# Gated cross-attention with a routed expert layer: bias add ahead of row sends, other send batches, plan pieces, normalisation by slot, products first

## The chip, the cores and the metric

The kernel runs on one core of a Trainium2 chip. The metric is device time in microseconds (us), the median of repeated runs, lower is better. A profile is one further execution, recorded by the hardware profiler; it has a span (first to last instruction) and its own device time. Engines: TensorE (PE, with PEld for its weight loads), VectorE (DVE), ScalarE (ACT), GpSimd (POOL), and SyncE (SP), which only issues transfers.

## The reference

For 32 sequences of 128 rows and 128 columns (float32):

```
x  = x + tanh(g0) * xattn(ctx, layernorm(x), mask)     # 8 heads of 16; ctx is 32 x 128 x 256
x  = x + tanh(g1) * ffn(layernorm(x))
xattn: k, v from ctx (W_src), q from layernorm(x) (W_tgt), softmax(q k / 4) v with the mask,
       then [layernorm(x), update] @ W_out + b_out
ffn:   router of 8 experts, softmax, top 2 (weights renormalised), h = gelu(x @ w1[e]) (512 wide),
       y = h @ w2[e], sum of the two experts' y with their weights
```

The expert layer computes for each row only its two experts. Rows are therefore sorted by expert at run time.

## The kernel before, in words

**Two stages, one program.** The attention works through 32 sequences in 8 groups of 4. A step (g, k), g from 0 to 12 and k from 0 to 3, advances every stage of the pipeline by one sequence: the sequence of a stage is n = 4g + k - LAG, with lags from 4 (projections) over 5 and 6 (scores), 7 (products of the values, `LAG_PV`) to 8 (the outputs' transposes, `LAG_O`). Work per group follows at group lags: 3 (output projection, second layernorm), 4 (router), 5 (`LAG_SEND`: sends). The expert stage is a list of 71 slots of 128 rows of one expert each: transpose (slot n), first product (n + 2), second product (n + 4). Steps up to (9,1) run alone; from (9,2) on (`MIXED`) each step is followed by 2 or 3 slots (`PER_OF`): (9,2) by slots 0 to 2, (9,3) by 3 to 5, (10,0) by 6 to 8, and so on; the rest of the slots follow alone.

**Order.** Each engine has its own instruction list in program order, written by a function `step` (and `slot`) per engine; semaphores are the only connection. An instruction that waits holds up all that stands behind it on its engine.

**One step on TensorE** (L1495 on): transposes of the outputs of one sequence (L1501), transpose and projections of another (L1510 to L1528), at k = 0 the ranks of a routed group (L1428 to L1445), the turn of the row maxima (L1493), and then at k = 0 the transposes of the second layernorm's rows (L1540, into `ps_tail`, which must wait until VectorE has read the ranks: its instruction `before`, L1064) and of the attention outputs (L1550); at k = 1 the output projection (L1557), at k = 2 the router (L1566). The products of the values (L1581) and the score block (L1460 to L1479) end the step. The turn waits for both maxima of the step (L1247: first of the far half of the heads, then, after `rsum` and `on`, of the near half); the near one overwrites a buffer that ScalarE's exponent (L751) of the sequence before must have read.

**ScalarE** copies results out of PSUM (kT L788, vals L791, x2nT L799, onT L805, oT L812), takes the exponents, normalises (L745 first, L739 second layernorm), and in the expert stage copies xt (L846) and applies GELU (L855).

**GpSimd** builds the key blocks (L595, L598), computes rs and mr of both layernorms (L605 to L618), adds the output bias to the group's rows of `xs` (L642; for the first group L624) for which VectorE's residual add (L1310) of the next step waits, makes the mask's penalties (L634), and issues the sends: for each group 8 indirect transfers (L657) that scatter its rows into the experts' regions of `rows` in DRAM, `scatter(G, sends)` with batches of two per step by the table `SENDS`: sends 0 and 1 at (G+5, 1), 2 and 3 at (G+5, 2), 4 and 5 at (G+5, 3), 6 and 7 at (G+6, 0). At k = 3 the bias add stands behind the sends. The groups 5 to 7 are sent from slots. Results go back by further indirect transfers (L675).

**The plan.** VectorE computes at run time which slot serves which expert, in three stages: slots 0 to 24 from the first four groups, 25 to 40 from six, the rest from all. `first_plan` has five pieces, one each at (8,0), (8,1), (8,2), (8,3), (9,0); piece 2 (`pass_ends`) is L1120 and L1124, piece 3 (`sum_up`) L1136 and L1137. SyncE issues the slots' loads (`xg`, L543): load 0 needs the first plan and all sends of the groups 0 to 3.

**Second layernorm.** `normalise_again(G, ...)` gives four instructions on ScalarE at (g, 3), ahead of the near exponent; for group 7 alone (`AHEAD`, g = 10) they are issued one by one in the slots 14 to 17. L1540 of the next step needs all four.

Of the kernel before, what the change touches and what calls it, by code (L numbers as in the profile page):

```python
# [10 lines left out]
ALU = mybir.AluOpType  # L11
# [4 lines left out]
T = 128  # L16
# [57 lines left out]

SENDS = (range(6, 8), range(0, 2), range(2, 4), range(4, 6))
KQ = 4
BOXES = 3
# [32 lines left out]

AHEAD = (10, 2)
PAIRS_AT = (5, 11, 12, 13, 15, 17, 22, 24, 26)
# [21 lines left out]
def sequence(g, k, lag):  # L134

    n = GROUP * g + (k - lag)
    if isinstance(n, int) and not 0 <= n < BATCH:
        return None
    return n


def group(g, lag):
    n = g - lag
    if isinstance(n, int) and not 0 <= n < GROUPS:
        return None
    return n
# [20 lines left out]
def gated_cross_attention_moe(nc, x, ctxT, mask, weights, vectors, w1, w2, ident_c, tables_c,  # L167
                              integers_c, rows, picked, out):
    with ExitStack() as stack:
# [409 lines left out]
        def _(pool):  # L579
# [6 lines left out]
            def step(g, k):  # L586
# [32 lines left out]
                G = group(g, 0)  # L619
                if k == 3 and G == 0:  # L620
                    if isinstance(g, int) and g == 0:
                        pool.wait_ge(s_setup, 3)
                    pool.wait_ge(s_xn, GROUP * G + GROUP)
                    nc.gpsimd.tensor_tensor(  # L624
                        xs[:, bass.ds(GROUP * G, GROUP), :], xs[:, bass.ds(GROUP * G, GROUP), :],
                        bout_g[:, :].unsqueeze(1).broadcast_to([128, GROUP, D]),
                        ALU.add).then_inc(s_xb, 1)
# [9 lines left out]
                if G is not None and G <= STAGES[0]:  # L637
                    scatter(G, SENDS[k])
                G = group(g, 0)
                if k == 3 and G is not None and G > 0:  # L640
                    pool.wait_ge(s_xn, GROUP * G + GROUP)
                    nc.gpsimd.tensor_tensor(  # L642
                        xs[:, bass.ds(GROUP * G, GROUP), :], xs[:, bass.ds(GROUP * G, GROUP), :],
                        bout_g[:, :].unsqueeze(1).broadcast_to([128, GROUP, D]),
                        ALU.add).then_inc(s_xb, 1)

            def scatter(G, sends):

                i = outbox(G)[0]
                if sends[0] == 0:  # L650
                    pool.wait_ge(s_pos, POS * G + POS)
                    pool.wait_ge(s_rt, ROUTE * G + ROUTE)
                    pool.wait_ge(s_xr, G + 1)
                    settled()
                for t in sends:
                    pick, b = divmod(t, GROUP)
                    nc.gpsimd.indirect_dma_start(  # L657
                        out=rows, out_offset=bass.IndirectOffsetOnAxis(
                            ap=posi[:, i, pick, b:b + 1], axis=0),
                        in_=xr[:, i, pick, b, :], in_offset=None).then_inc(s_send[i], 16)  # L660
# [50 lines left out]
        def _(act):  # L711
# [37 lines left out]
            def exponent(n, banks, heads_of, done):  # L749
# [4 lines left out]
                    bias=pencol[:, bass.ds(n, 1)]).then_inc(done, 1)  # L754

            def step(g, k):
                n = sequence(g, k, LAG_PROJ)
# [26 lines left out]
                if n is not None:  # L784
                    act.wait_ge(s_proj, n + 1)
                    wait(act, s_kblkr, n - 3)
                    wait(act, s_kblk, n - 3)
                    nc.scalar.activation(kT[:, (k - LAG_PROJ) % KQ, :], ps_proj[:, 0:T], ACT.Identity,  # L788
                                         bias=bkey).then_inc(s_k, 1)
                    wait(act, s_pv, n - 3)  # L790
                    nc.scalar.activation(  # L791
                        vals[:, (k - LAG_PROJ) % 4, :, 0:HD],
                        ps_proj[:, 2 * T:3 * T].rearrange("p (h c) -> p h c", c=HD),
                        ACT.Copy).then_inc(s_v, 1)
                G = group(g, LAG_ROUTE)
                if k == 0 and G is not None:
# [9 lines left out]
                if k > 0:  # L806
                    copy_maxima(g, k)
                n = sequence(g, k, LAG_PV)
                if n is not None:
                    act.wait_ge(s_pv, n + 1)  # L810
                    wait(act, s_o, n)
                    nc.scalar.activation(flat(oT[:, :, :]), ps_o[:, 0:2 * T], ACT.Copy).then_inc(s_oT, 1)  # L812
                G = group(g, 0)
# [7 lines left out]
                G = group(g, LAG_OUT)  # L821
                if k == 3 and G is not None and g != AHEAD[0]:
                    normalise_again(G, range(GROUP))
# [17 lines left out]
            def slot(n):  # L841
# [10 lines left out]
                if j is not None:  # L852
# [3 lines left out]
                                         ACT.Gelu).then_inc(f_gelu, 1)  # L856
                b = n - slot_at(*AHEAD) - 2
                if 0 <= b < GROUP:
                    normalise_again(AHEAD[0] - LAG_OUT, (b,))
                G, late = divmod(n - ADD_FROM - 3, 2)  # L860
# [19 lines left out]
        def _(dve):  # L880
# [371 lines left out]
            def step(g, k):  # L1252
                n = sequence(g, k, LAG_SCORE + 1)
                if n is not None:
                    dve.wait_ge(s_sc, n + 1)
                    if n == 0:
                        dve.wait_ge(s_zero, 3)
                    highest(n, FAR, s_max_far)
                n = sequence(g, k, LAG_O)
                if n is not None:  # L1260
# [11 lines left out]
                n = sequence(g, k, LAG_SCORE + 1)  # L1272
                if n is not None:
                    wait(dve, s_exp_near, n)
                    highest(n, NEAR, s_max)
# [54 lines left out]
                if k == 2 and G is not None:  # L1330
                    parts[:] = routing(G)
                    parts[0]()
                piece = {(8, 0): 0, (8, 1): 1, (8, 2): 2, (8, 3): 3, (9, 0): 4}.get((g, k))
                if piece is not None:
                    first_pieces[piece]()
# [67 lines left out]
        def _(pe):  # L1403
# [81 lines left out]
            def turn_maxima(g, k):  # L1485

                n = sequence(g, k, LAG_ST)
                if n is not None:
# [5 lines left out]
                                        ident[:, :]).then_inc(s_maxTp, 1)  # L1494

            def step(g, k):
                n = sequence(g, k, LAG_O)
# [34 lines left out]
                if k == 0:  # L1532
                    turn_maxima(g, k)
                G = group(g, LAG_ROUTE)
                if k == 0 and G is not None:
# [33 lines left out]
                if k > 0:  # L1569
                    turn_maxima(g, k)  # L1570
                n = sequence(g, k, LAG_PV)
                if n is not None:
                    r = (k - LAG_PV) % 2
                    if isinstance(n, int) and n == 0:
                        pe.wait_ge(s_pool0, 1)
                    pe.wait_ge(s_exp, n + 1)
                    pe.wait_ge(s_v, n + 1)
                    wait(pe, s_on, n)
                    for h in range(HEADS):
                        q = h % QUADS  # L1580
                        last = nc.tensor.matmul(  # L1581
                            ps_o[VPAD * q:VPAD * (q + 1), (h // QUADS) * T:(h // QUADS + 1) * T],
                            vals[:, (k - LAG_PV) % 4, h, :], probT[:, r, h, :], start=True, stop=True)
                    last.then_inc(s_pv, 1)
                n, m = sequence(g, k, LAG_SCORE), sequence(g, k, LAG_ST)
# [105 lines left out]
```

## Time and profile before

| | |
|---|---|
| runs | 326.61 us median of 3 (326.29 to 327.12) |
| profiled execution | 324.83 us, span 323.0 us |
| granted TensorE clock | 1.0 in every stretch up to the last matmul |
| busy | PE 291.3 us (90%), PEld 262.8, DVE 210.2, ACT 193.9, POOL 220.7 |
| attention alone | 0 to about 164 us |
| attention's end mixed with slots | 164 to about 220 us |
| slots alone | to 307 us |
| gather, last adds and stores | 307 to 323 us |

Times of instructions are counted from the start of the span. A row of a timeline gives the start, the length, the engine, the line of the kernel, and in brackets how long the engine stood idle before and what ended that. "issue" as a releaser means that the profile shows no instruction that ended just then. Matmuls overlap, so a small gap may not show as idle time.

### The profile page before, as it was taken

Reading aid. Unit: us, or ns where it says so; the run is one execution under the profiler, and the core shown is the slowest. Engines: PE = TensorE matmul, PEld = TensorE weight load, DVE = VectorE, ACT = ScalarE, POOL = GpSimd, SP = SyncE. Lnnn points to the kernel's source line nnn. Section 1 sums busy time; section 2 is a strip of 40 time slices with the busy share of each in tenths; the row PEclk is TensorE's granted clock in tenths of the full one; section 3 lists DMA queues with packets and bytes.
Section 4 is the critical chain, followed back from the end, with each engine's and each line's share of the span. In section 5 each row is a group of like instructions: output and inputs, shape, how many; then the busy total and the mean of one; then the engine's idle time right before and its main releaser. Section 6 shows DMA issues by size and latency. Waiting matters only on the chain.

```text
span 323.0 us, 10882 instructions
## 1 busy us (share of the span) xinstructions
PE 291.3 (90%) x3529; PEld 262.8 (81%) x3529; DVE 210.2 (65%) x886; ACT 193.9 (60%) x502; POOL 220.7 (68%) x301
## 2 busy tenths in 40 slices
PE   8799999998989999897788999999999999999920
PEld 3687787887879778776568998989999999999920
DVE  2758677698888868689567897359533443335653
ACT  3486869788797877867675448474444444444400
POOL 3745445443788888888555788788788888756860
PEclk9999999999999999999999999999999999999995
DMA  6635703113141211860234213213434333349346
GB/s 205 193 116 161 224 30 94 44 33 82 54 133 35 68 58 44 237 161 27 61 95 117 70 53 86 85 60 90 112 92 112 99 98 99 86 147 297 100 134 195
DMA packets 41236, 34.60 MB, mean 107 GB/s; under 512 B 5044, under 2 KB 36950, under 8 KB 41184
## 3 DMA queue, kind: packets, MB, share of 16 engines
q1 hardware_dynamic: 32608, 23.10, 25.8%
q0 software_dynamic: 4320, 8.47, 7.9%
q10 hardware_dynamic: 4256, 2.36, 2.5%
q8 instruction: 30, 0.49, 0.7%
q14 instruction: 22, 0.18, 0.2%
HBM read 22.35 MB, written 12.01 MB: 106 GB/s over the span
## 4 chain that ended last, share of the span: by engine, by line
PE 51%; POOL 23%; issue 14%; DVE 4%; ACT 3%; DMA 2%; POOLq 0%; ACTq 0%; DVEq 0%; SPq 0%
PE ps_sc L1622 16%; POOL rows L657 11%; PE ps_proj L1635 8%; PE ps_o L1635 7%; POOL kblk L598 3%; PE ps_o L1581 2%; POOL kblkr L595 2%; PE ps_proj L1516 2%; PE ps_o L1419 2%; PE ps_proj L1519 2%; POOL picked L675 2%; PE ps_sc L1465 2%; POOL xs L642 2%; POOL rs L614 2%; PE ps_sc L1460 1%
## 5 line engine op out<-in xcount | busy, mean ns | idle before, releaser
L675 POOL DMA_INDIRECT picked<-yo,xg x71 | 71.6, 1008 | 16.2 <-issue 11.2
L1622 PE MATMUL ps_sc<-xt,w1c 128*128 128x128 f32 x568 | 75.3, 276 | 1.8 <-ACT xt L846 1.2
L657 POOL DMA_INDIRECT rows<-xr,posi x64 | 63.4, 990 | 18.0 <-issue 17.4
L1622 PEld LDWEIGHTS ps_sc<-xt,w1c 128*128 128x128 f32 x568 | 69.0, 192 | 2.5 <-ACT xt L846 1.5
L855 ACT ACTIVATE probT<-ps_sc 128x512 f32<-128x512 f32 x71 | 42.4, 597 | 41.3 <-PE ps_sc L1622 41.3
L751 ACT ACTIVATE probT<-ps_sc,pencol 128x512 f32<-128x512 f32 x64 | 43.6, 683 | 18.7 <-PE ps_sc L1479 12.1
L1247 DVE TENSOR_REDUCE rowmax<-ps_sc 128x4 f32<-128x512 f32 x64 | 43.8, 685 | 13.9 <-PE ps_sc L1479 11.9
L595 POOL TENSOR_TENSOR kblkr<-kT,headcol 128x256 fp32r<-128x256 f32 x32 | 19.7, 616 | 35.5 <-ACT kT L788 35.2
L1635 PE MATMUL ps_proj<-w2s,probT 128*128 x288 | 38.0, 275 | 0.0
L1635 PE MATMUL ps_o<-w2s,probT 128*128 x280 | 37.0, 275 | 0.0
L1357 DVE COPY w1c<-w1s 128x512 f32 x71 | 32.0, 454 | 5.5 <-issue 3.4
L1635 PEld LDWEIGHTS ps_proj<-w2s,probT 128*128 128x128 f32 x288 | 35.0, 192 | 0.0
L1635 PEld LDWEIGHTS ps_o<-w2s,probT 128*128 128x128 f32 x280 | 34.1, 192 | 0.0
L1377 DVE TENSOR_SCALAR yo<-ps_o,xg 128x128 f32<-128x128 f32 x35 | 12.3, 350 | 27.0 <-PE ps_o L1635 26.6
L1377 DVE TENSOR_SCALAR yo<-ps_proj,xg 128x128 f32<-128x128 f32 x36 | 12.6, 350 | 25.5 <-PE ps_proj L1635 25.2
L1465 PE MATMUL ps_sc<-qT,kblk 32*128 32x128 f32 x512 | 21.3, 282 | 0.0
L1516 PE MATMUL ps_proj<-ctxs,wts 128*128 128x128 f32 x128 | 19.8, 277 | 1.5 <-DVE xs L1310 1.5
L1581 PE MATMUL ps_o<-probT,vals 128*32 128x128 f32 x512 | 20.6, 279 | 0.1
L598 POOL TENSOR_TENSOR kblk<-kT,headcol 128x256 f32<-128x256 f32 x32 | 19.7, 616 | 0.0
L1519 PE MATMUL ps_proj<-wts,ctxs 128*128 128x128 f32 x128 | 19.5, 275 | 0.0
L1305 DVE SCALAR_TENSOR_TENSOR qT<-ps_proj,wts,maskbc 128x128 f32<-128x128 f32 x32 | 11.1, 348 | 12.6 <-ACT vals L791 10.0
L1516 PEld LDWEIGHTS ps_proj<-ctxs,wts 128*128 128x128 f32 x128 | 16.9, 192 | 1.9 <-issue 1.9
(169 smaller groups left out, 605.9 us busy)
## 6 DMA issues: line engine op xcount, KB each, us to landing
xg<-rows SPq DMA_DIRECT2D x71, 65.0 KB, 1.9
ctxs<-ctxT SPq DMA_DIRECT2D x32, 128.0 KB, 2.2
xs<-x SPq DMA_DIRECT2D x8, 256.0 KB, 3.6
maskbc<-mask SPq DMA_DIRECT2D x8, 256.0 KB, 4.1
w1s<-w SPq DMA_DIRECT2D x4, 512.0 KB, 3.8
w2s<-w SPq DMA_DIRECT2D x8, 256.0 KB, 4.8
maskbc<-picked SPq DMA_DIRECT2D x4, 512.0 KB, 5.8
out<-xs ACTq DMA_DIRECT2D x6, 256.0 KB, 2.3
```

Source lines behind the costliest of these rows:

```text
L598: nc.gpsimd.tensor_tensor(kblk[:, r, :, :], kT[:, r, :].unsqueeze(1).broadcast_to([128, PAIR, T]), headcol[:, :].unsqueeze(2).broadcast_to ...
L657: nc.gpsimd.indirect_dma_start(out=rows, out_offset=bass.IndirectOffsetOnAxis(ap=posi[:, i, pick, b:b + 1], axis=0), in_=xr[:, i, pick, b, ...
L675: nc.gpsimd.indirect_dma_start(out=picked, out_offset=bass.IndirectOffsetOnAxis(ap=xg[:, r, D + 1:D + 2].bitcast(I32), axis=0), in_=yo[:, ...
L751: nc.scalar.activation(probT[:, n % 2, heads_of, :].rearrange("p (j i) t -> p j (i t)", i=PAIR), scores[:, banks, SOURCE], ACT.Exp, scale= ...
L855: nc.scalar.activation(hid[:, j % DEEP, :, :], heads(ps_score[j % DEEP][:, :]), ACT.Gelu).then_inc(f_gelu, 1)
L1247: nc.vector.tensor_reduce(rowmax[:, n % 2, banks, 0:PAIR], scores[:, banks, TARGET].rearrange("p j (i s) -> p j i s", i=PAIR), AX.X, ALU.m ...
L1357: nc.vector.tensor_copy(w1c[:, j % DEEP, :], w1s[:, turn["experts"][j % REGS], :].rearrange("p o h -> p (o h)")).then_inc(f_w1, 1)
L1465: last = nc.tensor.matmul(scores[:, j, i * T:(i + 1) * T], kblk[strip, m % KQ, i, :], qT[strip, m % KQ, :], start=False, stop=n is None an ...
L1516: nc.tensor.matmul(ps_proj[:, 0:T], wsrc[:, c, 0:D], ctxs[:, b, c, :], start=(c == 0), stop=(c == FCH - 1))
L1581: last = nc.tensor.matmul(ps_o[VPAD * q:VPAD * (q + 1), (h // QUADS) * T:(h // QUADS + 1) * T], vals[:, (k - LAG_PV) % 4, h, :], probT[:, ...
L1622: last = nc.tensor.matmul(ps_score[j % DEEP][:, c * 128:(c + 1) * 128], w1c[:, j % DEEP, c * 128:(c + 1) * 128], xt[:, j % XRING, :], star ...
L1635: last = nc.tensor.matmul(ps_y[j % 2][:, 0:D], hid[:, j % DEEP, c, :], w2s[:, e, c, :].rearrange("p o d -> p (o d)"), start=(c == 0), stop ...
```

## The change

- **Bias.** GpSimd's bias add at k = 3 comes ahead of the penalties and the sends for every group, as it did for group 0.
- **Sends.** Group 3 is sent 3, 2 and 3 at (8,1), (8,2), (8,3) and none at (9,0); group 4 is sent 6 at (9,1), 2 at (9,2), none at (9,3) and (10,0).
- **Plan.** Pieces 1 and 2 of the first plan both stand at (8,1), pieces 3 and 4 both at (9,0).
- **Normalisation.** The second normalisation of group 6 leaves (9,3) and is issued one sequence at a time in slots 2 to 5, as that of group 7 was in slots 14 to 17.
- **Products.** At k = 0 TensorE issues the products of the values right behind the turn of the maxima, ahead of L1540 and L1550, and ScalarE copies them (oT) ahead of x2nT and onT.
- **Maxima.** At g = 9 VectorE's near maxima come ahead of `rsum` and `on`.

`copy_outputs` and `products` hold the former lines of oT and of the products, unchanged. Of the removed bias add of the groups 1 to 7 only the first lines are shown.

```diff
+SENDS_OF = {3: (range(0), range(0, 3), range(3, 5), range(5, 8)),
+            4: (range(0), range(0, 6), range(6, 8), range(0))}
-AHEAD = (10, 2)
...
@@ GpSimd, step @@
-                if k == 3 and G == 0:
+                if k == 3 and G is not None:
...
                     pool.wait_ge(s_xn, GROUP * G + GROUP)
                     nc.gpsimd.tensor_tensor(xs_of_group, xs_of_group, bout_g_broadcast, ALU.add).then_inc(s_xb, 1)
...
                 if G is not None and G <= STAGES[0]:
-                    scatter(G, SENDS[k])
-                G = group(g, 0)
-                if k == 3 and G is not None and G > 0:
...
+                    scatter(G, SENDS_OF.get(G, SENDS)[k])
             def scatter(G, sends):
-                if sends[0] == 0:
+                if 0 in sends:
...
@@ ScalarE, step and slot @@
+                if k == 0:
+                    copy_outputs(g, k)
                 G = group(g, LAG_ROUTE)
                 if k == 0 and G is not None:
                     act.wait_ge(s_x2Tp, G + 1)
...
+                if k > 0:
+                    copy_outputs(g, k)
...
-                if k == 3 and G is not None and g != AHEAD[0]:
+                if k == 3 and G is not None and (g, 2) not in STEPS[MIXED:]:
                     normalise_again(G, range(GROUP))
...
-                b = n - slot_at(*AHEAD) - 2
-                if 0 <= b < GROUP:
-                    normalise_again(AHEAD[0] - LAG_OUT, (b,))
+                for g, k in STEPS[MIXED:]:
+                    b = n - slot_at(g, k) - 2
+                    if k == 2 and group(g, LAG_OUT) is not None and 0 <= b < GROUP:
+                        normalise_again(g - LAG_OUT, (b,))
...
@@ VectorE, step @@
+                n = sequence(g, k, LAG_SCORE + 1)
+                if n is not None and g > GROUPS:
+                    wait(dve, s_exp_near, n)
+                    highest(n, NEAR, s_max)
                 n = sequence(g, k, LAG_O)
...
-                if n is not None:
+                if n is not None and g <= GROUPS:
                     wait(dve, s_exp_near, n)
                     highest(n, NEAR, s_max)
...
-                piece = {(8, 0): 0, (8, 1): 1, (8, 2): 2, (8, 3): 3, (9, 0): 4}.get((g, k))
-                if piece is not None:
+                for piece in {(8, 0): (0,), (8, 1): (1, 2), (9, 0): (3, 4)}.get((g, k), ()):
                     first_pieces[piece]()
...
@@ TensorE, step @@
                 if k == 0:
                     turn_maxima(g, k)
+                    products(g, k)
...
                 if k > 0:
                     turn_maxima(g, k)
+                if k > 0:
+                    products(g, k)
```

## Rows read from the trace of the kernel before

**Rows 1.** Table of stretches: length, busy us (instructions) of PE, PEld, DVE, ACT, POOL; clock; DMA.
```profile
177.00:307.00 130.00, 128.66 (x1161) 127.99 (x1160) 71.09 (x255) 64.65 (x142) 101.16 (x132) 1.00 0.36 105
```

**Rows 2.** Waits of TensorE from 20 to 164 us; the columns: total, times, longest (us).
```profile
PE ps_xT L1493 <- issue: 5.5, 7, 2.2
...
PE ps_tail L1540 <- DVE before L1064: 1.6, 5, 0.5
...
PE ps_xT L1550 <- ACT maxT L721: 0.5, 1, 0.5
```

**Rows 3.** Timeline of step (7,0); the columns: start us, us, instruction [idle before <-releaser].
```profile
114.33 0.63 PE L1540 MATMUL ps_tail<-ident,xr 128*128 128x128 f32 x4 [0.28 <-DVE before L1064]
...
115.32 0.65 PE L1581 MATMUL ps_o<-probT,vals 128*32 128x128 f32 x16
...
115.90 0.45 PE L1460 MATMUL ps_sc<-maxT,pick 32*128 32x128 f32 x8
```

**Rows 4.** Timeline from 114 to 122 us: the bias add and what follows.
```profile
114.66 0.96 POOL L657 DMA_INDIRECT rows<-xr,posi  x1 [0.30 <-issue]
...
115.64 1.29 POOL L642 TENSOR_TENSOR xs<-xs,bout_g 128x512 f32<-128x512 f32 x1
...
116.96 0.29 DVE L1310 TENSOR_TENSOR xs<-ps_proj,xs 128x128 f32<-128x128 f32 x1 [1.73 <-POOL xs L642]
...
120.24 0.30 PE L1493 MATMUL ps_xT<-ident,rowmax 128*128 128x128 f32 x1 [0.38 <-issue]
...
121.24 0.30 PEld L1460 LDWEIGHTS ps_sc<-maxT,pick 32*128 32x128 f32 x8 [0.40 <-ACT maxT L721]
```

**Rows 5.** Waits of GpSimd from 83 to 160 us.
```profile
POOL rows L657 <- issue: 8.8, 32, 0.6
...
POOL kblkr L595 <- ACT kT L788: 0.2, 1, 0.2
```

**Rows 6.** Timeline around 72.5 us: GpSimd and VectorE.
```profile
72.52 1.27 POOL L642 TENSOR_TENSOR xs<-xs,bout_g 128x512 f32<-128x512 f32 x1
...
72.57 1.24 DVE L1022 SCALAR_TENSOR_TENSOR tsum<-topp 128x4 f32<-128x4 f32 x1
```

**Rows 7.** Timeline, steps (8,2) to (9,0).
```profile
147.56 0.37 DVE L1124 TENSOR_TENSOR gone<-past,hops 128x200 f32<-128x200 f32 x1
...
149.79 0.30 PE L1493 MATMUL ps_xT<-ident,rowmax 128*128 128x128 f32 x1 [0.87 <-issue]
...
152.56 0.67 ACT L751 ACTIVATE probT<-ps_sc,pencol 128x512 f32<-128x512 f32 x1
...
153.84 0.68 DVE L1247 TENSOR_REDUCE rowmax<-ps_sc 128x4 f32<-128x512 f32 x1
...
154.62 0.30 PE L1493 MATMUL ps_xT<-ident,rowmax 128*128 128x128 f32 x1 [2.16 <-issue]
```

**Rows 8.** Timeline from 151 to 165 us: sends, first load, slot 0.
```profile
151.86 1.01 POOL L657 DMA_INDIRECT rows<-xr,posi  x1 [0.17 <-issue]
...
155.70 0.96 POOL L657 DMA_INDIRECT rows<-xr,posi  x1 [0.30 <-issue]
...
159.71 18.78 SPq L543 DMA_DIRECT2D xg<-rows  x22
...
164.02 0.30 PE L1613 MATMUL ps_xT<-ident,xg 128*128 128x128 f32 x1 [0.33 <-issue]
...
164.21 1.04 POOL L614 TENSOR_TENSOR rs<-ve,minus_half 128x4 f32<-128x4 f32 x1 [4.94 <-DVE ve L906]
```

**Rows 9.** DMA issues on the page; the columns: size each, median us to landing.
```profile
xg<-rows SPq DMA_DIRECT2D x71, 65.0 KB, 1.9
```

**Rows 10.** Timeline from 171 to 173 us: ScalarE and TensorE.
```profile
171.81 0.60 ACT L855 ACTIVATE probT<-ps_sc 128x512 f32<-128x512 f32 x1 [0.99 <-PE ps_sc L1622]
...
172.51 0.60 PE L1540 MATMUL ps_tail<-ident,xr 128*128 128x128 f32 x4
```

**Rows 11.** Timeline at 130.46 us: ScalarE.
```profile
130.46 1.64 ACT L739 ACTIVATE xr<-xs,mr,rs 128x128 f32<-128x128 f32 x4
```

More of the change, by code:

```diff
@@ L637, in step @@
                 if G is not None and G <= STAGES[0]:
-                    scatter(G, SENDS[k])
-                G = group(g, 0)
-                if k == 3 and G is not None and G > 0:
[L641 to L645, printed above, removed]
+                    scatter(G, SENDS_OF.get(G, SENDS)[k])
             def scatter(G, sends):
                 i = outbox(G)[0]
-                if sends[0] == 0:
+                if 0 in sends:
                     pool.wait_ge(s_pos, POS * G + POS)
@@ L754, in exponent, with copy_outputs @@
                     bias=pencol[:, bass.ds(n, 1)]).then_inc(done, 1)
+            def copy_outputs(g, k):
+                n = sequence(g, k, LAG_PV)
+                if n is not None:
+                    act.wait_ge(s_pv, n + 1)
+                    wait(act, s_o, n)
+                    nc.scalar.activation(flat(oT[:, :, :]), ps_o[:, 0:2 * T], ACT.Copy).then_inc(s_oT, 1)
             def step(g, k):
@@ L807, in step @@
                     copy_maxima(g, k)
-                n = sequence(g, k, LAG_PV)
-                if n is not None:
-                    act.wait_ge(s_pv, n + 1)
-                    wait(act, s_o, n)
-                    nc.scalar.activation(flat(oT[:, :, :]), ps_o[:, 0:2 * T], ACT.Copy).then_inc(s_oT, 1)
+                if k > 0:
+                    copy_outputs(g, k)
                 G = group(g, 0)
@@ L1272, in step @@
                 n = sequence(g, k, LAG_SCORE + 1)
-                if n is not None:
+                if n is not None and g <= GROUPS:
                     wait(dve, s_exp_near, n)
@@ L1494, in turn_maxima, with products @@
                                         ident[:, :]).then_inc(s_maxTp, 1)
+            def products(g, k):
+                n = sequence(g, k, LAG_PV)
+                if n is not None:
+                    r = (k - LAG_PV) % 2
+                    if isinstance(n, int) and n == 0:
+                        pe.wait_ge(s_pool0, 1)
+                    pe.wait_ge(s_exp, n + 1)
+                    pe.wait_ge(s_v, n + 1)
+                    wait(pe, s_on, n)
+                    for h in range(HEADS):
+                        q = h % QUADS
+                        last = nc.tensor.matmul(
+                            ps_o[VPAD * q:VPAD * (q + 1), (h // QUADS) * T:(h // QUADS + 1) * T],
+                            vals[:, (k - LAG_PV) % 4, h, :], probT[:, r, h, :], start=True, stop=True)
+                    last.then_inc(s_pv, 1)
             def step(g, k):
@@ L1570, in step @@
                     turn_maxima(g, k)
[L1571 to L1584, printed above, removed]
+                if k > 0:
+                    products(g, k)
                 n, m = sequence(g, k, LAG_SCORE), sequence(g, k, LAG_ST)
```

## The prediction

> **What bounds the kernel now.** I read the table of stretches first. From 177 to 307 us TensorE is busy 128.66 of 130 us, so that stage shrinks only by starting earlier [rows 1]. The view of TensorE's waits between 20 and 164 us says what it stands for before that: 5.5 us ahead of the turn of the maxima (L1493), 1.6 in five pieces at the transposes L1540, 0.5 once at L1550 [rows 2]. The timelines then show each wait by itself. The end moves one for one with what goes there, provided that the first slot's rows (below) arrive in time.
>
> **Products first (steps k = 0).** At (7,0) TensorE stands 0.28 us at L1540 for VectorE's `before`, and the products, which wait for nothing there, come only after eight transposes, at 115.32; the next work starts at 115.90, so they fill 0.58 us [rows 3]. That covers each of the five stalls (0.5 at most) and the one at L1550 in (3,0). Counting (9,0) apart (0.28, below): 1.6 - 0.3 + 0.5 = 1.8 us gained. ScalarE copies the outputs while L1540 runs, and x2nT and onT follow as before; its cover is its wait for the score block. Without that cover the price is one copy, 0.4 us. The added wait of the products on `on` ahead of L1540 lies behind the turn's own wait on a later VectorE instruction, so it is free for g up to 8.
>
> **Bias ahead of the sends.** In (6,3) the second send starts at 114.66 after 0.30 of issue, 1.26 us each, then the bias add from 115.64 to 116.93, for which VectorE waits 1.73 us at L1310; its next maxima are late, TensorE idles 0.38 at 120.24, and the weight loads of the score block wait 0.40 for maxT, 0.2 more than in most steps [rows 4]. The same happens in three groups, with 0.66 at 140.41 and none at (6,1) for the turn. With two sends off ahead of it, the bias stands at 113.0 to 114.3 and VectorE's wait (115.2 wanted) is gone. Gain 0.4 + 0.7 + 3 x 0.2 = 1.7. But GpSimd itself is full: between 83 and 160 us it waited 0.2 us for ScalarE, the rest of its gaps being its own issue (8.8 us over 32 sends) [rows 5]. The work per group is unchanged, so each us that TensorE gains finds GpSimd that much later. By (7,3) TensorE is 0.3 + 0.2 + 0.3 + 0.6 = 1.4 us ahead of it; the third bias (135.37 before) would end at 134.1 and is wanted at 135.0 - 1.4 = 133.6, so it is 0.5 late again. I count 1.7 - 0.45 = 1.25. Bounds: 0 (GpSimd's lag eats it) to 1.7.
>
> **A price of the same move.** At 72.57 VectorE's `tsum`, both inputs in SBUF, ran 1.24 us and ended with the bias add that ran from 72.52 to 73.79 [rows 6]. The bias at 113.0 to 114.3 lies on `tw` and `before`, which have two SBUF inputs as well and stand ahead of L1540, wanted at 114.33 [rows 3]. If they restart at 114.3, L1540 is ready near 114.8, while the products occupy TensorE until about 114.55: 0.25 us lost, three times 0.75. Bounds: 0 (no overlap) to 1.0 each (the whole add less 0.3 of cover). I take 0.75, as in the row two such instructions met in this way.
> The Trainium skill (SBUF — State Buffer, section Who interferes with whom) states that a VectorE instruction with two SBUF inputs and a GpSimd instruction that reads SBUF exclude each other for the whole instruction. The `tsum` row agrees (1.24 us); by the rule all three adds collide and the sum is the one below, without it 0.75 us more would be gained.
>
> **First plan at other steps.** The 0.37 us instruction `gone` and its like before it hold the maxima of (8,3) back, and TensorE idles 0.87 at 149.79 [rows 7]. They move to (8,1), in front of the maxima of (8,2), where TensorE had no stall and VectorE no slack: up to 2 x 0.37 = 0.74 lost there, 0.87 gained at (8,3), net +0.1 (bounds -0.7 to +0.9). The two sums leave (8,3) too; the plan is still written some 3 us before the first load.
>
> **(9,0) and (9,1).** TensorE idles 2.16 us before the turn at 154.62. VectorE's near maxima run 153.84 to 154.52; they may start only when ScalarE's exponent from 152.56 (0.67) is done, at 153.23 [rows 7]. Put ahead of `on` they start at 153.25: 0.6 us gained, not 2.16, because ScalarE still has four normalisations before that exponent. The products now wait for `on`, 0.5 us after the near maxima, so at (9,1) only 0.1 is left, which I drop. Bounds: 0 to 1.3.
>
> **Sends and the first load.** The last send of group 3 runs 155.70 to 156.66, load 0 is issued at 159.71, and slot 0 is transposed at 164.02 [rows 8]; the load lands 1.9 us after issue [rows 9]. So slot 0 could start at 161.6, and 2.4 us is the cap unless GpSimd is earlier. It is: its full stretch starts after the gains of (3,0) to (5,0), about 1.1 us, and the sends of group 3 keep their place in its queue (three at (8,1), two, three, none at (9,0)). Cap 3.5 us; the gains so far stay under it. At (9,1) six sends of group 4 follow in a row, 6 x 1.27 = 7.6 us, from about 155.5 to 163.1. Behind them waits `rs` for group 6, which started at 164.21 after 4.94 us of idleness [rows 8]; VectorE now offers its input near 161.2, so it starts 1.9 us late against that, yet earlier in absolute time than before. With 1.5 us for `rs` and `mr2` it is done at 164.7; slot 2's normalisation wants it behind a GELU that ends about 164.6. I cost this at 0. Two sends fewer stand behind the first results after 173; nothing of TensorE waits for those.
>
> **Normalising per slot.** Four normalisations, 1.64 us together [rows 11], leave (9,3) and go one each behind the GELUs of slots 2 to 5. TensorE did not stall on the old block. The last one now follows the GELU of 171.81 (0.60), ends near 172.9, and L1540, which ran at 172.51, waits [rows 10]: 0.45 us lost. Bounds: 0 to 0.9.
>
> **Sum.** 1.8 + 1.25 - 0.75 + 0.1 + 0.6 - 0.45 = 2.55, say 2.6 us. The profiled execution took 324.83 us (span 323.0 and 1.83 around it), so it would become 322.2. The median shown is 326.61, 1.78 above it; I carry the difference over: 324.0. If all upper bounds held, the first load caps the gain near 4 us (322.6).
>
> **Rivals.**
> 1. GpSimd is the bound. It waits under 1 us for others in 77 us [rows 5], and its work is not reduced; all that needs its results then moves with it. Only what is gained before its full stretch (1.1 us) counts, less the slots' 0.45: 0.7 us, 325.9. Against it: `kblkr`, its commonest result, is wanted only a step later.
> 2. Given back at the join. TensorE stops at 164 for register loads, the table load and w1c, and again at 173 for x2nT. If attention ends 2 us earlier but rows, `rs` or the weights come at their old times, 0 to 0.4 remains: 326.4. For it: load 0 follows GpSimd's sends, not TensorE. Against it: 2.4 us lay between landing and use.
> 3. Slower: the six sends in one batch. If a send costs more in a row of six than the 1.27 us it costs in pairs, `rs` and `mr2` of group 6 come late. ScalarE's in-order queue meets the first normalisation in slot 2, at 164.6; from there every us that `mr2` is late holds xt of slot 3 and the next GELU, and TensorE behind them. At 1.8 us a send the six end at 166.3 and `mr2` at 167.8, 3.2 us late: 3.2 + 0.45 against 3.0 gained before the slots, 327.3. It decides from 1.7 us a send on. Against it: four sends in a row ran from 151.86 to 156.66 at 1.28 us each [rows 8].
>
> **Chances.** Forecast 0.6, rival 1 0.18, rival 2 0.13, rival 3 0.09. A change of 0.3% (1 us) is about what a measurement can tell from none. Faster takes the forecast nearly whole and a third of rival 1: 0.65; slower is rival 3 and a little: 0.1; the rest, 0.25, is the same. The forecast's own range is 322.6 to 325.2; with rivals 1 and 2 taken in it reaches 326.5.
>
> **What would show it.** Right: L1540 follows the products with no stall on `before`, or with one of about 0.2 where the bias overlaps `tw`; L1310 no longer waits over 1 us for the bias in (6,0) and (7,0); the turn at (9,0) idles near 1.5 us; slot 0's transpose lies at 160.5 to 161.5; L1540 at (10,0) waits for ScalarE. A new stall at the turn of (8,2), up to 0.7, shows the moved plan pieces. Wrong: slot 0 at 163 or later, GpSimd's `mr2` awaited by ScalarE at (7,3) or in slot 2, or sends longer than 1.3 us in the row of six.

## The result: 0.67% slower

The changed kernel takes 328.68 us (median of 15 runs, 327.28 to 331.79); the ratio to the kernel before is 1.0067, 95% interval 1.0041 to 1.0093. Forecast were 324.0 us and a range of 322.6 to 326.5. A ratio leaves out runs that lie over 1.5% above the fastest run of their kernel; below this concerns e5 (two of twelve) and e9 (five of twelve). The profiled execution took 327.54 us, its span is 325.5 against 323.0.

The page shows first that TensorE has as many instructions as before (busy 291.3 us then), that VectorE is busy 7.6 us more (210.2 before), and that the clock row has one 7, where the page before has only nines up to the last slice:

```profile
span 325.5 us, 10883 instructions
...
PE 292.5 (90%) x3529; PEld 263.7 (81%) x3529; DVE 217.8 (67%) x886; ACT 194.4 (60%) x502; POOL 220.4 (68%) x301
...
PEclk9999999999999999999799999999999999999995
```

TensorE's waits between 20 and 164 us (total, times, longest) answer [rows 2]. The stalls ahead of the transposes (L1563 now) are gone, as forecast. In their place stands one that no row of before had: 4.4 us at the rank's first matmul (L1433), for VectorE's `sel_b`: 1.5 us at most in each of (6,0), (7,0), (8,0), 0.6 in (9,0).

```profile
PE ps_tail L1433 <- DVE sel_b L1027: 4.4, 4, 1.5
PE ps_xT L1498 <- issue: 4.2, 8, 0.8
PE ps_proj L1549 <- ACT xnT L763: 1.0, 2, 0.6
PE ps_xT L1498 <- DVE rowmax L1249: 1.0, 1, 1.0
```

The timelines of GpSimd, VectorE and TensorE around step (7,0) show why; they answer [rows 3, 4].

```profile
111.37 0.62 POOL L596 TENSOR_TENSOR kblkr<-kT,headcol 128x256 fp32r<-128x256 f32 x1
111.94 0.61 POOL L599 TENSOR_TENSOR kblk<-kT,headcol 128x256 f32<-128x256 f32 x1
112.52 1.26 POOL L625 TENSOR_TENSOR xs<-xs,bout_g 128x512 f32<-128x512 f32 x1
...
111.33 2.50 DVE L1022 TENSOR_TENSOR sel<-tables,topi 128x32 f32<-128x32 f32 x1
...
114.11 0.19 PE L1433 MATMUL ps_tail<-sel_b,strict_b 128*128 128x32 bf16 x1 [1.18 <-DVE sel_b L1027]
...
115.80 0.30 PE L1498 MATMUL ps_xT<-ident,rowmax 128*128 128x128 f32 x1 [0.83 <-issue]
...
117.19 0.28 DVE L1316 TENSOR_TENSOR xs<-ps_proj,xs 128x128 f32<-128x128 f32 x1
```

`kblkr`, `kblk` and the bias add now run on GpSimd with nothing between them, from 111.37 to 113.78. VectorE's second `sel`, both inputs in SBUF and some 0.2 us long by itself, starts at 111.33 and ends at 113.83: it stands for all three. `tsum` and `sel_b` queue behind it, TensorE stands 1.18 us for them, and 0.83 more at the turn, because VectorE's maxima are late as well. The Trainium skill (SBUF — State Buffer, section Who interferes with whom) says of a VectorE instruction with two SBUF inputs and a GpSimd instruction that reads SBUF that the second waits for the whole instruction; here it waited for three.

In the kernel before the two did not meet at this place at all: both `sel` were done 1 us before `kblkr` began.

```profile
110.76 0.29 DVE L1020 TENSOR_TENSOR sel<-tables,topi 128x32 f32<-128x32 f32 x2
...
111.99 0.62 POOL L595 TENSOR_TENSOR kblkr<-kT,headcol 128x256 fp32r<-128x256 f32 x1
```

The first of the three collisions, at (6,0), lengthens one that before had as well: `tsum` at 91 to 92 us stood 0.71 us there and stands 2.48 now. After it VectorE is late against GpSimd, and that brings `sel` onto `kblkr` in the next two groups: at (8,0) `kblkr` starts at 131.73 before and 131.75 now, the first `sel` at 130.48 and 131.58.

The last row of the longer timeline shows that the bias move also did what it was meant to: `xs` follows `qT` at once (1.73 us of waiting before). At 117.19 one of its two inputs is in PSUM, and though `kblkr` and `kblk` run beside it, it takes its usual 0.28 us.

Starts of the score block, from the timelines; difference to before in brackets (e3 and e11 are experiments below):

```
step       before   changed         e3              e11
(2,3)       35.69    35.47 (-0.2)
(5,3)       90.78    89.68 (-1.1)    89.80 (-1.0)    89.84 (-0.9)
(6,0)       96.86    97.22 (+0.4)    95.55 (-1.3)    95.61 (-1.3)
(7,0)      115.90   117.62 (+1.7)   114.60 (-1.3)   114.87 (-1.0)
(7,1)      121.24   122.13 (+0.9)   120.27 (-1.0)   119.38 (-1.9)
(8,0)      135.84   138.00 (+2.2)   134.36 (-1.5)   133.67 (-2.2)
(8,1)      141.41   142.61 (+1.2)   140.44 (-1.0)   138.18 (-3.2)
(8,2)      145.92   147.87 (+2.0)   144.95 (-1.0)   142.78 (-3.1)
(8,3)      150.60   151.95 (+1.4)   149.63 (-1.0)   148.16 (-2.4)
(9,0)      156.77   158.67 (+1.9)   155.48 (-1.3)   156.01 (-0.8)
(9,1)      160.71   162.86 (+2.2)   159.42 (-1.3)   161.59 (+0.9)
```

Up to (5,3) the change is ahead. (6,0), (7,0) and (8,0) then cost 1.5, 1.3 and 1.2 us, each against the step before it ((6,3) at +0.4 and (7,3) at +1.0 are not in the table), and (6,1), (7,1), (8,1) give back 0.1, 0.8 and 1.0, where the wait for the bias was.

The table of stretches (length, busy of PE, PEld, DVE, ACT, POOL, clock, DMA) has the second new thing. After 153 to 156 us, in which TensorE was busy 1.23 of 3 us, its granted clock is 0.5, that is 1.2 GHz, from 156.1 to 159.5. The last row answers [rows 1]: the stage from 177 us on is as it was.

```profile
153.00:156.00 3.00, 1.23 (x22) 0.70 (x18) 2.96 (x12) 2.72 (x7) 2.53 (x4) 1.00 0.14 44
156.00:160.00 4.00, 4.00 (x56) 3.25 (x53) 1.82 (x10) 1.59 (x4) 3.20 (x5) 0.57 0.18 54
...
177.00:307.00 130.00, 128.68 (x1162) 128.05 (x1161) 70.80 (x255) 65.15 (x145) 98.93 (x128) 1.00 0.35 103
```

This fall is not the difference between the kernels. Every run lists its mean granted clock: 0.974 over 29 runs of the kernel before (beside e5 to e8), 0.975 over the 15 of the changed one. The profile of before (0.986, 324.83 us) was of a run without a fall. At like clocks (means): near 0.980, 326.6 (5 runs) before and 327.5 (6) after; near 0.976, 326.8 (8) and 328.9 (6); near 0.965, 328.4 (5) and 331.4 (3).

### The profile page after: what moved, and what is told of

Read it like the earlier page. It is cut to its first block, busy times and chain, and to the rows that moved or that the text cites. A ratio compares the mean times of both kernels' runs of the same rounds, so it can differ in the third digit from the quotient of the medians.

```text
span 325.5 us, 10883 instructions
## 1 busy us (share of the span) xinstructions
PE 292.5 (90%) x3529; PEld 263.7 (81%) x3529; DVE 217.8 (67%) x886; ACT 194.4 (60%) x502; POOL 220.4 (68%) x301
## 4 chain that ended last, share of the span: by engine, by line
PE 71%; DVE 13%; issue 8%; ACT 4%; DMA 2%; POOL 1%; DVEq 0%; POOLq 0%; ACTq 0%; SPq 0%
PE ps_sc L1633 19%; PE ps_proj L1646 9%; PE ps_o L1646 9%; PE ps_o L1513 4%; PE ps_sc L1470 3%; PE ps_proj L1538 3%; PE ps_proj L1541 3%; PE ps_sc L1465 2%; DVE rowmax L1249 2%; PE ps_proj L1549 2%; DVE sel L1022 2%; PE ps_o L1424 2%; PE ps_o L1523 2%; PE ps_proj L1550 2%; PE ps_tail L1580 2%
## 5 line engine op out<-in xcount | busy, mean ns | idle before, releaser
L664 POOL TENSOR_TENSOR pscratch<-minus_half 1x1 f32<-1x1 f32 x46 | 11.8, 257 | 12.7 <-DVE yo L1382 12.0
```

## Experiments

Theories: (1) the queue of three on GpSimd; (2) TensorE's lower clock; (3) the rest of the change (send batches, plan, normalisation). Medians are given with the ratio to the kernel before on the same chip (327.0 us for e1 to e8, 326.8 for e9 to e12).

### e1: the change with the bias behind the sends

```diff
-                if k == 3 and G is not None:
+                if k == 3 and G == 0:
...
                     scatter(G, SENDS_OF.get(G, SENDS)[k])
+                G = group(g, 0)
+                if k == 3 and G is not None and G > 0:
+                    pool.wait_ge(s_xn, GROUP * G + GROUP)
+                    nc.gpsimd.tensor_tensor(
+                        xs[:, bass.ds(GROUP * G, GROUP), :], xs[:, bass.ds(GROUP * G, GROUP), :],
+                        bout_g[:, :].unsqueeze(1).broadcast_to([128, GROUP, D]),
+                        ALU.add).then_inc(s_xb, 1)
```

> The changed kernel with the bias add put back behind the sends of its step; all else of the change stays. Theory 1 (queue of three: kblkr, kblk and the bias add run back to back on GpSimd, VectorE's sel or tsum stands for all three, 2.5 us, and TensorE waits at the rank): the waits at the rank, 4.4 us in four pieces, go (under 0.3 in all), sel and tsum are under 1 us each, and the time is about 325.3, some 3.4 below the changed kernel and 1.3 below the kernel before. Theory 2 (TensorE's granted clock: the stretch at 156 to 160 us at the lower level, whatever brought it, is the loss): the stretch is still there and the time stays at 327 to 329. Theory 3 (the six sends of group 4 in a row, the moved plan pieces, the normalisations per slot): nothing of it is undone here, so the time stays near 328.5.

325.68 us, ratio 0.9946 (0.9926 to 0.9967). Of TensorE's 4.4 us at the rank 0.6 are left, in one piece:

```profile
PE ps_tail L1440 <- DVE sel_b L1034: 0.6, 1, 0.6
```

Against the changed kernel's 1.0067 that is 1.2%, some 4 us (3.0 between the medians), for the place of one instruction. At like clocks it is 2.1 us (near 0.980: mean 325.5 of six runs against 327.5) to 2.4 (near 0.976: 326.4 of four against 328.9); the rest goes with the clock, as three of the changed kernel's 15 runs are at 0.965 and none of e1's twelve. Theory 3 falls as the main cause. Theory 2 does too: the fall of the clock in the changed kernel's trace is still there (154 to 157.4 us, 0.5), and the kernel is faster than the one before.

### e2: the bias move alone

```diff
-                if k == 3 and G == 0:
+                if k == 3 and G is not None:
...
-                if k == 3 and G is not None and G > 0:
-                    pool.wait_ge(s_xn, GROUP * G + GROUP)
...
-                        ALU.add).then_inc(s_xb, 1)
```

> The kernel before with the bias add put ahead of the sends, and nothing else of the change. Theory 1: sel or tsum stands up to 2.5 us in groups 5 to 7, TensorE waits at the rank some 3 to 4.4 us in all and wins back about 1.9 at the next turns; time 328 to 329, the whole loss. Theory 2: slower only if a stretch at the lower clock appears. Theory 3: 326.6 or less, as the sends and the plan are those of before.

332.4 us, ratio 1.0146 (1.0104 to 1.0189): 3.4 us beyond the upper end expected. The stalls are as expected (below: 3.5 us at the rank). But (6,0), (6,1) lost 5.8 us, where the changed kernel lost 1.5 at (6,0). The stretches say why: in 92 to 95 us TensorE was busy 1.53 of 3 us, and from 95.8 to 106 the clock is 0.5.

```profile
PE ps_tail L1421 <- DVE sel_b L1018: 3.5, 3, 1.5
```

```profile
92.00:95.00 3.00, 1.53 (x18) 1.34 (x17) 3.00 (x4) 1.82 (x5) 2.81 (x5) 1.00 0.84 174
95.00:99.00 4.00, 3.04 (x21) 2.28 (x21) 3.30 (x16) 2.18 (x6) 3.07 (x5) 0.60 0.30 88
99.00:106.00 7.00, 7.00 (x67) 6.27 (x68) 2.98 (x15) 3.77 (x9) 2.52 (x4) 0.50 0.06 19
```

Its six runs have a mean clock of 0.951 to 0.981; the one at 0.981 took 330.1, those at 0.951 took 334.7 and 334.9. The 330.1 are 3.5 us above the kernel before near 0.980, about what was expected of the stalls. So theory 1 holds, and theory 2 returns in part: in this trace the stall costs once more in the clock.

### e3: products first alone

```diff
                 if k == 0:
                     turn_maxima(g, k)
+                    products(g, k)
...
+                if k == 0:
+                    copy_outputs(g, k)
```

> The kernel before with values' products (and ScalarE's copy of them) first in the steps k = 0, and nothing else. Prediction's term: 1.8 us gained. From the changed kernel's trace up to 90 us, where it gained 0.9 over three steps, theory 1 expects 0.9 to 1.8 gained if the bias stays where it was: 324.8 to 325.7. Theory 2: products first empties TensorE's later stretch and brings the lower clock: 327 or more.

325.44 us, ratio 0.9939 (0.9915 to 0.9963). In the trace the lead is 1.3 us at slot 0, 0.1 of it from before the first products, and 1.3 at the last GELU. The transposes follow the products without a stall. The wait of `xs` for the bias, 1.73 us, is still there, and the lead shrinks by 0.3 to 0.5 behind it, at (6,1), (7,1) and (8,1).

```profile
113.00 0.65 PE L1515 MATMUL ps_o<-probT,vals 128*32 128x128 f32 x16
113.58 0.66 PE L1565 MATMUL ps_tail<-ident,xr 128*128 128x128 f32 x4
...
115.98 0.29 DVE L1317 TENSOR_TENSOR xs<-ps_proj,xs 128x128 f32<-128x128 f32 x1 [1.73 <-POOL xs L642]
```

### e4: the rest alone

```diff
+SENDS_OF = {3: (range(0), range(0, 3), range(3, 5), range(5, 8)),
+            4: (range(0), range(0, 6), range(6, 8), range(0))}
...
+                for piece in {(8, 0): (0,), (8, 1): (1, 2), (9, 0): (3, 4)}.get((g, k), ()):
```

(with the near maxima first and the normalisation per slot)

> The kernel before with the rest alone: send batches of groups 3 and 4, plan pieces at other steps, near maxima first from step (9,0), normalisation per slot; bias and products as before. Theory 1: 326 to 327, no difference that can be told; in the trace some 0.7 us lost at the turn of (8,2), 0.6 to 0.9 won at (8,3). Theory 3: 328 or more. Theory 2: 328 with a stretch at the lower clock near 156 us.

327.18 us, ratio 1.0012 (0.9986 to 1.0038): no difference. In its trace 0.7 us is lost at (8,2) and 0.4 won at (8,3), where 0.6 to 0.9 was expected, and 0.8 is lost at (9,0), 0.6 of it at the rank for `sel_b`. The three parts alone add to -0.61 + 1.46 + 0.12 = 0.97%, the whole is 0.67%.

### e5: the bias between the two sends

The next four start from e3.

```diff
                         in_=xr[:, i, pick, b, :], in_offset=None).then_inc(s_send[i], 16)
+                    if biased is not None and t == sends[0]:
+                        add_bias(biased)
```

> The kernel before with products first, and the bias add of groups 5 to 7 between the two sends of its step, not behind both. Theory 1 (a queue of three GpSimd instructions without a send between them holds VectorE's two-input instructions for all three): kblkr and kblk are now followed by a send, so sel and tsum stand 0.7 us at most, as with the bias behind both sends, and TensorE waits under 0.3 us at the rank, though the bias add is still ahead of a send. The bias ends 1.3 us earlier, the waits for xs go, and the time is 0.3 to 1 us below products first alone: 324.4 to 325.1. Rival 1b (any earlier place of the add costs, since VectorE's small instructions fill that stretch): sel, tw or before stand over 1 us in groups 5 to 7, and the time is 326 or more. Theory 2 (clock): where TensorE stands no longer than with products first alone, the runs' mean granted clock is the same (0.976 to 0.986).

326.8 us, ratio 0.9990 (0.9962 to 1.0017): 0.5% slower than e3, where 0.3 to 1 us faster was expected. Half of theory 1 holds: with a send behind `kblkr` and `kblk`, `sel`, `tsum` and `sel_b` stand 0.76 us at most in the three groups, and the rank has no stall. Rival 1b holds beside it: the add at 113.50 now meets `tw`, which runs as long as the add, and TensorE stands at the transposes, 2.9 us in three groups. This is the collision that the prediction had priced, at 0.25 us each; here it comes to the upper bound of 1.0 each. The mean clock of the twelve runs is 0.968 against 0.979 in e3, and in the trace a stretch at 0.5 follows the third stall (135.3 to 138.7 us). At like clocks (0.975 to 0.980) the five runs have a mean of 325.5 us, e3's four 325.6: what e5 lost between the medians goes with the clock.

```profile
113.50 1.27 POOL L642 TENSOR_TENSOR xs<-xs,bout_g 128x512 f32<-128x512 f32 x1
...
113.55 1.26 DVE L1046 TENSOR_TENSOR tw<-tinv,tgates 128x4 f32<-128x4 f32 x1
...
115.21 0.63 PE L1567 MATMUL ps_tail<-ident,xr 128*128 128x128 f32 x4 [0.80 <-DVE before L1073]
```

### e6: plan pieces

```diff
-                piece = {(8, 0): 0, (8, 1): 1, (8, 2): 2, (8, 3): 3, (9, 0): 4}.get((g, k))
+                for piece in {(8, 0): (0,), (8, 1): (1, 2), (9, 0): (3, 4)}.get((g, k), ()):
```

> The kernel before with products first and the plan pieces at the steps of the change. By the step table of the run with the rest alone: about 0.7 us lost at the turn of (8,2), 0.4 won back at (8,3), and some 0.5 more at (9,0) if the sums stand ahead of it: 0 to 0.5 us slower than products first alone, 325.4 to 325.9. Rival (the pieces are what makes the stretch from 154 us on fall to the lower clock): the fall shows in the profile and the time is 326.5 or more.

325.11 us, ratio 0.9929 (0.9906 to 0.9951): not to be told from e3. In the trace 0.70 us is lost at (8,2) and 0.71 won at (8,3). A fall of the clock is there from 154 to 157.4, against the rival's figure of 326.5 or more.

### e7: near maxima first

```diff
+                n = sequence(g, k, LAG_SCORE + 1)
+                if n is not None and g > GROUPS:
+                    wait(dve, s_exp_near, n)
+                    highest(n, NEAR, s_max)
```

> The kernel before with products first and the near maxima ahead of the outputs from step (9,0) on. Prediction's term: 0.6 us gained at the turn of (9,0), 0.1 at (9,1): 324.7 to 324.9 against 325.4 for products first alone, and TensorE's wait at that turn falls from 2.2 to some 1.6 us. Rival: the products, which now wait for the outputs behind the maxima, give 0.2 to 0.5 back at each of (9,0), (9,1): no difference, 325.4.

325.01 us, ratio 0.9926 (0.9906 to 0.9945). The median lies 0.1 us above what the term gave, but the interval holds e3 too. The turn of (9,0) came at 153.15 instead of 153.65 in e3, the products then waited 0.18 us.

### e8: send batches

```diff
-                    scatter(G, SENDS[k])
+                    scatter(G, SENDS_OF.get(G, SENDS)[k])
```

> The kernel before with products first and the send batches of groups 3 and 4 of the change. From the run with the rest alone, where sel at (8,3) stood 0.87 us beside kblkr and kblk and TensorE 0.6 us at the rank: if the batches put kblkr and kblk there, the same 0.6 is lost here, 325.9 to 326.1, and slot 0 is later by as much. Prediction's term (sends cost nothing): 325.4, no wait at the rank. Rival 3 of the prediction (the six in a row are slower than 1.27 us each): over 327; the row of six in the changed kernel, 1.26 us apart, speaks against it.

326.31 us, ratio 0.9985 (0.9959 to 1.0012): 0.9 us lost against e3, where theory 1 expected 0.5 to 0.7; but it is `nm` and `topp`, not `sel`, that `kblkr` now meets:

```profile
145.20 0.76 DVE L914 TENSOR_SCALAR nm<-mv 128x4 f32<-128x4 f32 x1
...
145.30 0.62 POOL L597 TENSOR_TENSOR kblkr<-kT,headcol 128x256 fp32r<-128x256 f32 x1
...
150.30 0.62 POOL L597 TENSOR_TENSOR kblkr<-kT,headcol 128x256 fp32r<-128x256 f32 x1
...
150.40 0.56 DVE L1018 TENSOR_TENSOR topp<-top,linv 128x8 f32<-128x8 f32 x1
```

`nm` took 0.25 us at the same time in e3. It has one SBUF input (`mv`, times a constant), so instructions with two are not the only ones that are held. The half us makes VectorE's maxima late, and the lead of 1.0 at (8,2) is 0.5 at (8,3), whose score block starts before `topp` does. `topp` (0.33 in e3) then costs TensorE 0.2 at the rank. At (9,0) and at the end the lead is 0.5.

### e9: e2 with TensorE's stall at the rank filled

```diff
+                if G in (1, 2, 3):
+                    pe.wait_ge(s_rt, ROUTE * G + 2)
+                    for i in range(FILL):
+                        nc.tensor.matmul(ps_tail[:, 128:256], ones_b[:, :], ones_b[:, :], start=True, stop=True)
```

> The kernel with the bias move alone (332.4 us; its runs had a mean granted clock of 0.951 to 0.981), and on TensorE 20 matmuls of 128 columns ahead of the rank of groups 1 to 3, whose results nothing reads: they fill the 1.5 us in which it stands there, and VectorE's collision stays as it is. Theory 2 in its weaker form (the stall costs twice, once as standing and once as the stretch at the lower clock that follows it): the mean clock rises to 0.975 to 0.98 and the time falls to about 330, the standing alone (3.4 over the kernel before). Theory 1 alone (the standing is all, the lower clock comes by itself): clock and time as with the bias move alone, 332 to 333.

330.39 us over all twelve runs, 1.1% above the kernel before; the ratio is 1.0052 (1.0011 to 1.0093). e2 has 1.0146. The mean clock of the twelve runs is 0.975, that of e2's six 0.963. The fill takes 1.28 us and leaves 0.36 of the 1.47 that TensorE stood:

```profile
93.03 1.28 PE L1422 MATMUL ps_tail<-ones_b 128*128 128x128 bf16 x20
94.68 0.19 PE L1426 MATMUL ps_tail<-sel_b,strict_b 128*128 128x32 bf16 x1 [0.36 <-DVE sel_b L1019]
```

VectorE's collision was unchanged (2.5 us in each group), and so was the time at which the rank could start. But no stretch at the lower clock follows at (6,0): at (6,1) this trace has lost 1.5 us against the kernel before, e2's 5.8. (One stands between 138 and 144 us, behind the third group.) What was won, 0.4% of the time over all runs and 0.9% by the ratios, fits the weaker form of theory 2: the clock behind the stalls was a part of e2's loss, the standing the rest. The runs scatter (326.18 to 332.51), so the share is rough. Two of them, 326.18 us at a clock of 0.976 and 327.12 at 0.970, lie 4 to 5 us below the others near their clock; they were not traced, and the reason is open.

### e10, e11, e12: better versions

e10 is e7 with the plan pieces of e6; e12 is e10 with the normalisation per slot:

```diff
-                if k == 3 and G is not None and g != AHEAD[0]:
+                if k == 3 and G is not None and (g, 2) not in STEPS[MIXED:]:
...
```

e11 is e7 with another order on GpSimd:

```diff
+BIAS_FIRST = ((6, 3), (7, 3))
...
+                early = (g, k) in BIAS_FIRST
+                if early:
+                    add_bias(g)
+                else:
+                    spread_keys(g, k)
...
+                    if early:
+                        scatter(G, SENDS[k][:1])
+                        spread_keys(g, k)
+                        scatter(G, SENDS[k][1:])
```

> Products first, the moved plan pieces and the near maxima first together; bias, sends and normalisation as before. If the single terms add (products first 325.4, with the plan pieces 325.1, with the near maxima 325.0): 324.6 to 324.8. If the near maxima, which the plan's sums of (9,0) now follow, and the lower clock at 154 us eat it: 325.1 to 325.5.

> Products first and near maxima first, and in (6,3) and (7,3) the bias add at the head of GpSimd's step, behind the last send of the step before, where VectorE's sel, tsum and sel_b are done; then a send, kblkr and kblk, the other send. Theory 1: VectorE's xs no longer waits 1.73 us for the bias (4.5 us in three groups now), no two-input instruction stands over 0.8 us, and the 0.3 to 0.5 us that TensorE loses after each such wait are won in two groups: 324.2 to 324.6 against 325.0. Rival: kblkr and kblk, 1.4 us later, come too late for the score block, which TensorE reaches 2.5 us behind their end now, or collide with tw and before: 325.5 or more.

> Products first, plan pieces, near maxima and the normalisation per slot, that is the change without its bias move and its send batches. Prediction's term for the normalisation: 0.45 us lost at the transposes of (10,0) against the same kernel without it (e10). The trace of the changed kernel shows 0.17 there: theory 1 expects 0 to 0.3 lost, 324.7 to 325.1. The send batches are what made the rest-alone kernel no faster: theory 1 expects this one to be 0.6 to 1 us below the changed kernel with the bias put behind (325.68).

e10: 325.02 us, 0.9938 (0.9907 to 0.9968); the terms do not add. e12: 325.52, 0.9946 (0.9921 to 0.9970); 0.5 more than e10, within the intervals, where 0 to 0.3 was expected. e12 is also e1 without the send batches; 0.6 to 1 us less than e1's 325.68 was expected, and it is 0.2, with the same ratio. So the 0.9 us that the batches cost next to e3 did not show next to e1. e11: 325.07, 0.9943 (0.9916 to 0.9971), not faster than e7. Its trace is the surprise: up to (8,2) it is 3.1 us ahead, the best of all, and no two-input instruction of VectorE meets the bias add in (6,3) or (7,3). Then TensorE stands 1.58 us at the turn of (8,3) (0.87 in e3), because the plan's `past` and `gone`, 0.36 and 0.37 us in e3, now meet `kblkr` and `kblk` (143.88 to 145.27): the same collision at one more place. From 148.4 the clock is 0.5 for 14 us:

```profile
144.05 0.75 DVE L1144 TENSOR_TENSOR past<-tables,ends 128x200 f32<-128x200 f32 x1
...
144.84 0.66 DVE L1148 TENSOR_TENSOR gone<-past,hops 128x200 f32<-128x200 f32 x1
```

```profile
144.00:148.00 4.00, 2.42 (x32) 2.10 (x32) 3.90 (x20) 2.56 (x8) 3.66 (x5) 1.00 0.06 17
148.00:152.00 4.00, 2.91 (x51) 2.05 (x40) 3.83 (x15) 2.49 (x6) 3.30 (x5) 0.55 0.10 33
...
156.00:162.00 6.00, 6.00 (x68) 4.93 (x71) 2.44 (x5) 3.04 (x6) 1.63 (x2) 0.50 0.29 72
```

At (9,1) the lead is gone, and it is 0.9 us behind. Its twelve runs have a mean clock of 0.970, those of e7 0.979; its fastest, at 0.975 to 0.977, took 324.2. e1, e3, e6, e7, e10, e11 and e12 all beat both kernels, the one before by 0.5 to 0.7%, and can't be told apart.

## Why the prediction was wrong

The step that failed is **A price of the same move**, and with it **Bias ahead of the sends**. The mechanism was named there, with the right row [rows 6], but at the wrong place and for the wrong length. I put the add at 113.0 to 114.3, onto `tw` and `before`; it ran from 112.52 to 113.78, straight behind `kblkr` and `kblk`. I treated it as one instruction of 1.27 us and did not ask what stands directly ahead of it on GpSimd: before, the queue of SBUF readers was two long and a send followed; after, three, 2.5 us. And I looked at the instructions that follow 113.0, not at `sel`, `tsum` and `sel_b` ahead of the rank, for the last of which TensorE waits, nor at where these would lie once the first stall had made VectorE late. Priced at 0.75 us in three groups, it cost 3.8 at the rank (1.47, 1.18 and 1.17). The sum had +0.5 for the two steps; by e1 they cost 2.1 to 2.4 us at like clocks, gain included, and 3 to 4 us over all runs. That the stall would also bring TensorE's lower clock is in no term of the sum.

Point by point, the others:

- **Products first, +1.8.** Right in kind: the stalls at L1540 went. 1.2 us in the trace of e3, 1.6 between the medians.
- **The gain of the bias move.** It came: `xs` waits no more, and 1.9 us were won at (6,1), (7,1), (8,1). It was paid in advance.
- **First plan, +0.1.** The two sides were sized rightly (0.7 lost at (8,2), 0.7 won at (8,3) in e6).
- **(9,0), +0.6.** 0.5 us at the turn in e7; in the time not to be told from none.
- **Sends, 0.** 0.9 us next to e3 (e8), though none next to e1 (e12), and not for the reason weighed: `rs` and `mr2` were in time, but fewer and more sends per step shift `kblkr` onto `nm` and `topp`, the same kind of collision again.
- **Normalising per slot, -0.45.** In the changed kernel's trace the lag of the GELUs grows by 0.37 from slot 0 (2.15) to slot 4 (2.52), though L1563 itself waits only 0.17. Right in size.
- **Median less profiled, 1.78.** I carried it over as a constant. It was the clock: the profiled run had 0.986, the runs beside the experiments 0.974.

The rivals fell. GpSimd is not the bound: e11 leaves its work as it was and is 3.1 us ahead at (8,2), where rival 1 allowed 1.1. e3 alone looks like rival 1, as what it gains at (6,0), (7,0) and (8,0) goes again one step later; but that is the wait for one late add, not the amount of work. In the changed kernel GpSimd waits 2.6 us for `kT`, against 0.2 [rows 5] (the view of before also has 0.8 us of waits for VectorE, which the prediction put down to issue).

```profile
POOL rows L651 <- issue: 9.1, 33, 0.6
POOL kblkr L596 <- ACT kT L790: 2.6, 6, 0.7
```

Nothing is given back at the join: e3's lead at slot 0 is its lead at the end. And the six sends in a row start 1.26 us apart (157.81 to 164.14); `rs` for group 6, at 166.37, waited 1.26 us for VectorE and for no send [rows 8].

Left open: what makes VectorE slip in between two GpSimd instructions or not. With a send behind `kblk`, `tsum` at 91 to 92 us ran after `kblkr` alone (0.7 us) in before and in e1; with the bias add behind, the same instruction at the same place waited for all three (2.5 us). I have no run that tells why. Not shown either is how much of the loss of one run is the standing and how much the clock; the shares above are from runs compared at like mean clocks. Nor did I try the changed order with the add left out.

## What to carry to other kernels

Before an instruction is moved on GpSimd, list what stands directly ahead of and behind it there without a send or a wait between: for VectorE's instructions with two SBUF inputs that whole queue can be one block (and `nm`, with one, was held too). Then look at which of those instructions TensorE waits for, at the time at which the block will lie, not at the time of the old place. One stall shifts VectorE against GpSimd, so the next groups have to be looked at again with that shift. Where TensorE is made to stand, count the stretch at the lower clock that may follow; a lead can be lost there too.

## What the runs showed of the hardware that I had not expected

- Three GpSimd instructions in a row (0.62, 0.61, 1.26 us) held one VectorE instruction for 2.50 us.
- An instruction with one SBUF input was held as well: `nm` 0.76 us beside `kblkr` in e8, 0.25 in e3.
- A send holds VectorE at some places and not at others. In e11 `tw` began 0.35 us after a send and stood to its end; in e3 it began 0.43 us after one and took its usual 0.16. What decides it is open.

```profile
112.50 0.98 POOL L674 DMA_INDIRECT rows<-xr,posi  x1 [0.17 <-issue]
...
112.85 0.63 DVE L1061 TENSOR_TENSOR tw<-tinv,tgates 128x4 f32<-128x4 f32 x1
```

```profile
112.36 1.01 POOL L657 DMA_INDIRECT rows<-xr,posi  x1 [0.17 <-issue]
...
112.79 0.16 DVE L1044 TENSOR_TENSOR tw<-tinv,tgates 128x4 f32<-128x4 f32 x1
```

- The granted clock of one and the same program differs from run to run: 0.965 to 0.986 for the kernel before, with 328.4 us at the one end and 325.1 at the other.
